# TensorE takes the negative branch of each pair of source tiles ahead of the positive one

## The reference, cut to what matters

```python
mask = A + jnp.eye(n, dtype=A.dtype) > 0
Wh = (H @ W).reshape(n, N_HEADS, D_K)
sl = jnp.einsum('nhd,hd->nh', Wh, a_l)
sr = jnp.einsum('nhd,hd->nh', Wh, a_r)
e = jax.nn.leaky_relu(sl[:, :, None] + sr.T[None, :, :], negative_slope=NEG_SLOPE)
e = jnp.where(mask[:, None, :], e, -jnp.inf)
alpha = jnp.nan_to_num(jax.nn.softmax(e, axis=2), nan=0.0)
out = jnp.einsum('nhm,mhd->nhd', alpha, Wh).reshape(n, OUT_DIM)
```

## Time and profile before

| | us |
|---|---|
| median of 3 runs | 906.07 |
| lowest and highest of them | 904.7 and 906.44 |
| the profiled execution | 906.77 |
| its span, first to last instruction | 905.2 |
| TensorE busy | 835.4 |
| VectorE busy | 723.5 |
| ScalarE busy | 695.5 |

### The profile page before, as it was taken

One profiled execution on the slowest core, in us unless ns is written; L12 is line 12 of the kernel. 1 busy time (PEld: TensorE's weight loads), 2 busy tenths in 40 slices (PEclk: granted clock), 3 DMA queues, 4 the chain that ended last, 5 costly groups with the idle time before them and its releaser, 6 DMA issues.

```text
span 905.2 us, 26463 instructions
## 1 busy us (share of the span) xinstructions
PE 835.4 (92%) x10273; PEld 668.7 (74%) x10273; DVE 723.5 (80%) x1367; ACT 695.5 (77%) x987; POOL 155.0 (17%) x221
## 2 busy tenths in 40 slices
PE   4998899999999998619999989999999999899996
PEld 3344455555555554319999989999999999899996
DVE  3897687878878786459888997888997889978885
ACT  2676566667676664369998998999998899989993
POOL 0111354645546453200000000000000000000000
PEclk9999999999999999859999999999999999999998
DMA  7346777788787879140041011221100410112011
GB/s 214 113 142 215 275 276 294 285 302 297 289 310 285 317 285 198 42 125 26 0 93 47 0 47 46 44 49 47 46 14 32 93 47 4 42 47 47 0 24 35
DMA packets 74873, 115.30 MB, mean 127 GB/s; under 512 B 55552, under 2 KB 57472, under 8 KB 66656
## 3 DMA queue, kind: packets, MB, share of 16 engines
q1 hardware_dynamic: 63344, 93.14, 31.6%
q0 software_dynamic: 7376, 20.85, 7.3%
q10 hardware_dynamic: 4128, 1.05, 0.6%
HBM read 98.17 MB, written 16.85 MB: 127 GB/s over the span
## 4 chain that ended last, share of the span: by engine, by line
PE 41%; ACT 7%; DVE 7%; issue 2%; DMA 0%; DVEq 0%; ACTq 0%
PE acc L952 41%; ACT sgn L979 5%; DVE sgn L1068 1%; DVE pos L1076 1%; DVE val L1102 1%; DVE total L1109 1%; DVE sgn L1058 1%; ACT total L997 1%; DVE vtmp L1094 1%; DMA srow<-s_scratch 0%; ACT val L989 0%; DVE yout L1140 0%; ACT ey L1002 0%; DVE ey L1135 0%; DVE total L1114 0%
## 5 line engine op out<-in xcount | busy, mean ns | idle before, releaser
L952 PE MATMUL acc<-val,pos 128*128 128x130 f16 x4096 | 482.3, 219 | 24.2 <-DVE val L1102 15.0
L952 PE MATMUL acc<-val,sgn 128*128 128x130 f16 x4096 | 482.4, 221 | 0.0
L952 PEld LDWEIGHTS acc<-val,pos 128*128 128x128 fp8e4 x4096 | 401.0, 98 | 27.2 <-issue 26.7
L979 ACT ACTIVATE sgn<-srow,rbias 128x1024 int8<-128x1024 f32 x384 | 404.4, 1169 | 2.8 <-DMA srow<-s_scratch 2.8
L952 PEld LDWEIGHTS acc<-val,sgn 128*128 128x128 fp8e4 x4096 | 397.0, 97 | 0.0
L430 PE MATMUL ps_a<-g,mT 128*128 128x512 f16 x1024 | 236.9, 386 | 2.5 <-DVE mT L696 2.5
L1068 DVE SCALAR_TENSOR_TENSOR sgn<-sgn,mask 128x1024 int32<-128x1024 int32 x128 | 156.4, 1222 | 45.1 <-ACT sgn L979 44.7
L430 PEld LDWEIGHTS ps_a<-g,mT 128*128 128x128 fp8e4 x1024 | 101.6, 99 | 114.1 <-issue 10.0
L533 ACT ACTIVATE junk<-bits 128x2048 uint8<-128x2048 uint8 x64 | 122.2, 1910 | 70.8 <-DVE bits L685 66.1
L1076 DVE TENSOR_SCALAR pos<-sgn 128x1024 int32<-128x1024 int32 x128 | 88.1, 689 | 18.9 <-PE acc L952 17.4
L1058 DVE TENSOR_SCALAR sgn<-srow,rbias 128x1024 uint8<-128x1024 f32 x128 | 96.0, 750 | 3.3 <-DMA srow<-s_scratch 3.3
(11 more groups left out here) (104 smaller groups left out, 615.9 us busy)
## 6 DMA issues: line engine op xcount, KB each, us to landing
stage<-in_adj SPq DMA_DIRECT2D x64, 1024.0 KB, 6.8
srow<-s_scratch SPq DMA_DIRECT2D x16, 512.0 KB, 4.7
mask<-in_x SPq DMA_DIRECT2D x16, 256.0 KB, 2.8
own_scratch<-mask POOLq DMA_DIRECT2D x16, 256.0 KB, 3.1
xt<-in_x POOLq DMA_DIRECT2D x32, 128.0 KB, 3.1
own<-own_scratch POOLq DMA_DIRECT2D x32, 128.0 KB, 5.5
x_scratch<-x POOLq DMA_DIRECT2D x32, 128.0 KB, 2.2
x1s<-x_scratch SPq DMA_DIRECT2D x16, 256.0 KB, 3.5
```

The lines of the kernel that those rows point to most:

```text
L952: last = nc.tensor.matmul(acc[j][:, br * VBLK:(br + 1) * VBLK], bytes_of(m[:, j * (P // 2):(j + 1) * (P // 2)])[:, b, :], val[:, 2 * k + b ...
L979: nc.scalar.activation(sign_bytes(sgn, k, b), srow[:, gr % 2, :], ACT.Sign, bias=rbias[:, 0, gr // NS, 2 * k + b:2 * k + b + 1]).then_inc( ...
```

## The change

Only TensorE's part of `layer1` changes. For each pair `q` it now waits for `z_ready`, goes over the eight banks with the negative products of both double tiles of the pair, four matmuls in each bank, then waits for `pos_ready` and goes over the eight banks with the positive products. The wait for a free bank (`plus_ready`) stands ahead of each bank's first negative product of pair 0. The matmul that starts a bank afresh (`start`) is now the first negative one. `pe_pair` and `pe_bank` are counted by the last positive products.

```diff
+            def branch(q, j, br, ring, size):
+                for k in (2 * q, 2 * q + 1):
+                    for b in range(2):
+                        last = nc.tensor.matmul(
+                            acc[j][:, br * VBLK:(br + 1) * VBLK],
+                            bytes_of(ring[:, k % size, j * (P // 2):(j + 1) * (P // 2)])[:, b, :],
+                            val[:, 2 * k + b, br * VBLK:(br + 1) * VBLK],
+                            start=br == 1 and k == 0 and b == 0, stop=k == NK - 1 and b == 1,
+                            skip_group_check=True)
+                return last
+
+            z32 = sgn[:, :, :].bitcast(I32)
             with pe.Fori(0, NG) as gr:
-                for k in range(NK):
-                    if k % CH == 0:
-                        pe.wait_ge(val_ready, gr // NS * (NCH * 2) + (k // CH + 1) * 2)
-                    if k % 2 == 0:
-                        pe.wait_ge(pos_ready, gr * NQ + (k // 2 + 1))
-                        hold(pe, waits_passed)
+                for q in range(NQ):
+                    if 2 * q % CH == 0:
+                        pe.wait_ge(val_ready, gr // NS * (NCH * 2) + (2 * q // CH + 1) * 2)
+                    pe.wait_ge(z_ready, gr * NQ + (q + 1))
+                    hold(pe, waits_passed)
                     for j in range(NJ):
-                        if k == 0:
+                        if q == 0:
                             pe.wait_ge(plus_ready, gr * NJ + (j + 1))
                             hold(pe, waits_passed)
-                        for b in range(2):
-                            first = k == 0 and b == 0
-                            final = k == NK - 1 and b == 1
-                            for br, m in enumerate((pos[:, k % PR, :], sgn[:, k % ZR, :].bitcast(I32))):
-                                last = nc.tensor.matmul(
-                                    acc[j][:, br * VBLK:(br + 1) * VBLK],
-                                    bytes_of(m[:, j * (P // 2):(j + 1) * (P // 2)])[:, b, :],
-                                    val[:, 2 * k + b, br * VBLK:(br + 1) * VBLK],
-                                    start=first and br == 0, stop=final, skip_group_check=True)
-                        if k == NK - 1:
+                        branch(q, j, 1, z32, ZR)
+                    pe.wait_ge(pos_ready, gr * NQ + (q + 1))
+                    hold(pe, waits_passed)
+                    for j in range(NJ):
+                        last = branch(q, j, 0, pos, PR)
+                        if q == NQ - 1:
                             last.then_inc(pe_bank, 1)
-                    if k % 2 == 1 and k < NK - 1:
+                    if q < NQ - 1:
                         last.then_inc(pe_pair, 1)
```

## The result

| | before | after |
|---|---|---|
| median of the runs, us | 905.43 (4 runs, 904.7 to 906.44) | 893.84 (4 runs, 890.09 to 894.53) |
| ratio of the runs, 95% interval | | 0.9866 (0.9834 to 0.9899) |
| the profiled execution, us | 906.77 | 890.09 |
| its span, us | 905.2 | 888.4 |
| the changed loop, from the start of its first matmul to the end of its last, us | 492.47 | 479.94 |

The change is 1.3% faster; 905.2 us had been forecast and 901.8 to 907.8 us as the range. A second set of six runs of the changed kernel gave 893.12 us and a ratio of 0.9859 (0.9834 to 0.9885).

What follows compares the result with a forecast made beforehand. TensorE was taken to bound the kernel, with 12.4 us of waiting in L952. From the 906.07 us median, 3.8 us won less two clock falls at 1.45 us gave -0.9 us, 905.2 us; range 901.8 to 907.8 us.

Steps and rivals of the forecast that it cites:

- What bounds the kernel: TensorE, busy 92% of the span; L952 takes 492.5 us, of which waiting costs 12.4 us.
- the 12.4 us of stops: Waiting in groups 3 and 4, 7 and 8, 11 and 12 of L952, 4.15 us per stretch.
- the 58.4 ns: TensorE's pace per matmul in L952 where nobody holds it up, from group 1's 29.89 us over 512 matmuls.
- The passed waits at nothing: The 128 added waits for `pos` with their increments in L952 cost nothing; bounded from above at 18 us.
- The stretch of groups 3 and 4: 1.86 us won in group 3 turns into idle before VectorE's bank read; 1.26 us won per stretch, 3.8 us in all.
- the 1.26 us that had been worked out: Gain per stretch from the early negative halves in group 4: 1.06 us at pair 1 and 0.20 us at pair 3.
- The clock: The new 2.59 us idle ahead of groups 4, 8 and 12 may drop TensorE to 1.2 GHz, 1.45 us per fall.
- Two falls in three: Forecast within rival 2: clock falls in two of three stretches, 905.2 us; rival 2, two or all three, chance 0.50.
- The order of the matmuls, taken at nothing: In L952, neither repeating nor changing PSUM columns between matmuls has a price, judged from L449 and L416; 0 us.
- Rival 4: Faster by much: the order restores L416's step in L952, 13 us less, 892 us; chance 0.04.
- 12.4 - 8.6 us from the stops: Of 12.4 us waiting in the three stretches, 8.6 us stay as VectorE's; 3.8 us are won.

Runs made afterwards that it cites:

- The padded kernels: Blocks of `val` 136 elements apart in place of 130: on the kernel before 896.76 us, ratio 0.9895; on the changed kernel 893.42 us, ratio 0.9849.
- the run with one block of columns: Kernel before, but from the second double tile on all matmuls of a bank add into columns 0 to 129 (sums wrong); loop 492.22 us.

## Why the prediction was wrong

- **What bounds the kernel.** Right, and it named its own gap: little beyond the 12.4 us of stops could come, "unless the new order alters the 58.4 ns". It did, by 1.5 ns.
- **The passed waits at nothing.** Right: 128 more waits and increments, and group 1 is shorter, not longer. The padded kernels, 29.05 us with them and 29.04 us without, leave nothing for them.
- **The stretch of groups 3 and 4.** Right in mechanism. The stops for `pos` went, the restart stayed at VectorE's read (32.57 us after the start of group 3, forecast 32.52), and the idle ahead of it is 2.48 us by the timeline, forecast 2.4. One stop that the forecast had just missed remained, 0.66 us at 517.37, because TensorE comes to pair 7 sooner with the cheaper step. Group 8 fell by 31.41 - 29.31 = 2.10 us. Taken as 512 x 1.5 ns = 0.78 us for the step and 1.3 us for the early start, that fits the 1.26 us that had been worked out. The split is arithmetic and not a measurement: the order without the early start brought only 31.41 - 30.92 = 0.49 us, as the stops for `pos` took up the rest. The step wins nothing in groups 3, 7 and 11, whose length is VectorE's.
- **The clock.** Right in kind and price: the new idle costs the clock its level in some of the cases, and a fall costs 30.84 - 29.31 = 1.53 us (1.45 forecast). Two falls in three had been forecast; one in three came in the profiled execution, and 4 in 9 over the traces with this idle.
- **The order of the matmuls, taken at nothing.** This is the step that failed. The forecast put the term at 0; it is 8.0 us outside the stretches and some 2.3 us in groups 4, 8 and 12, about 10 us in all, and it carried the time out of the range. With the order alone changed the loop fell by 7.1 us, with the padding alone by 9.7 us. Rival 4 had the effect, a size near it (13 us) and nearly the time (892 us), with a chance of 0.04, but it hung on the changing of columns in PSUM, which turned out to cost nothing. The reasoning against it was that L449 and L416, one repeating its columns and one changing them, both run at the plain pace. They were a fair test for PSUM, and the run with one block of columns confirmed that PSUM has no part in it. But they were no test for the operand that streams in: their slices of 264 and 128 two-byte elements are 528 and 256 bytes long, multiples of 16, while those of L952 are 260 bytes. The prediction itself put L952 1.6 ns above L416's step; I saw the difference and did not ask which operand of L952 was unlike those of the other two.

The sum, had the term been right: 12.4 - 8.6 us from the stops, 10 us from the step, less one or two falls of the clock at 1.5 us each, is 10.8 to 12.3 us; 11.6 us were measured (905.43 - 893.84). Of the 11.4 us by which the forecast of 905.2 us missed, about 10 are this one term.

## What to carry to other kernels

When one line of matmuls runs above the plain pace that other lines of the same trace keep, look at the addresses of its moving operand, matmul by matmul, before calling its order neutral: here a pad of 6 elements or a swap of two loops gave the pace that the reordering gave. Check each "no cost" against a row that has the same feature in the operand in question, not in another one. And time won ahead of a wait for another engine's queue only becomes idle time, as the 2.48 us ahead of group 4 did, which then can cost the clock its level.

## What the runs showed of the hardware

- A matmul whose moving operand begins in the same 16 bytes of a partition in which that of the matmul before ended takes some 2 ns more on the mean (2.0 to 2.3 ns in pairs 1 to 7 of three spacings, 1.8 to 2.6 ns by whole groups). Without it, 130 columns go at a mean of 56.7 ns; with it in three of four, at 58.4 ns. Neither the ring of the weights nor the block of columns in PSUM changed it.
- An idle of TensorE of 2.5 us in this loop was followed by a stretch at 1.2 GHz in 4 of 9 cases. In the one shown it began 1.26 us after the work had, and it cost 1.5 us (30.84 us in place of 29.31).
- Why the loop begins anywhere between 399.1 and 407.4 us, behind the same first stage, was not looked into. In the two traces of the changed kernel it makes 4.1 of the 5.8 us between their spans (888.4 and 894.2 us).
